# An attention stage whose inverse roots come from one GpSimd power, with the low parts of k made one tile later and in two halves

## The chip, the cores and the metric

The kernel runs on 1 core of one Trainium2 chip. The metric is the device time of one execution in microseconds (us), median of the runs shown; lower is better. The engines are named as the profile names them: PE is TensorE (PEld its weight loads), DVE is VectorE, ACT is ScalarE, POOL is GpSimd, and SP is SyncE, which issues most DMAs.

## The reference, cut to what matters

The whole program is a small network: attention, a mixture of 8 experts, a linear recurrence over the context, and a mixture of 64 experts with two shared ones. The change lies in the first part only:

```python
x = x + jnp.tanh(g_xattn[0]) * _L0_xattn_ref(_layernorm(x, axis=-1), ctx_2048, ctx_2048)
x = x + jnp.tanh(g_ffn[0]) * _L0_ffn_ref(_layernorm(x, axis=-1), L0_ffn_w_gate, ...)

def _layernorm(x, axis=-1, eps=1e-05):
    m = jnp.mean(x, axis=axis, keepdims=True)
    v = jnp.var(x, axis=axis, keepdims=True)
    return (x - m) / jnp.sqrt(v + eps)

def _L0_xattn_ref(q, k, v):            # q, k, v: (4, 512, 512); 8 heads of 64 rows
    attn = jnp.einsum('bct,bcs->bts', qh * scale, kh * scale)
    attn = jax.nn.softmax(attn, axis=-1)
    out = jnp.einsum('bts,bcs->bct', attn, vh)
```

There are 2048 rows of x, 16 tiles of 128 rows. Each tile is normalised, attends, is added back, is normalised again, and its rows are sent to the two experts that a small gate picks.

## The kernel before

The function `attention` holds the stage. It takes the 16 tiles one after another; a tile is 128 rows of x, which are two heads of 64 rows. Every engine runs its own loop over steps i, and in step i the engines work on several tiles at once:

- **PE** computes in step i, in four blocks b of 128 keys, the scores of tile i (L474, L483), the weighted values (L491), and for the next tile i+1 eight "rough" score products m = 0 to 7 (L498), from which only the row maximum is taken. All eight use one PSUM bank, `pM`, so rough m+1 can't start before DVE has read rough m. In between stand the transposes of the normalised tile (L549), those of the values (L554), and the gate's small matmuls (L513, L514, L562). The order of block 0 is: scores, L483, L513 and L514, values of the tile before, rough 0, transposes of `xn`.
- **DVE** takes the negated maximum of each rough product (L661), in the order m = 0 to 7. Between these stand the two halves of a reciprocal (L712), after m = 0 and after m = 1; after m = 3 the statistics of two tiles, of tile i+3 (L719, for the first normalisation) and of tile i-1 (L722, for the second); after m = 5 and 6 the choice of experts (L666 to L681). At the end of the step DVE makes the low parts of q for tile i+2 (L739, two halves, tile `q_parts`), and at the beginning of the next one it computes the slots of a tile's rows (`place`, L687 to L695).
- **ACT** takes the exponentials (L584), copies the softmax sums into `attn` (L590, L591), and at the end of the step rounds q and k to their high parts (L612, L616, tile `k_hi`) and writes the normalised tile `xn` (L622).
- **POOL** goes through an unrolled list: it scatters the rows of tile i-3 by two indirect DMAs (L397), makes q of tile i+2 (L404), finishes the attention of tile i-1 with a product and a sum (L410, L412), turns two variances into inverse roots (L92 to L98), writes the factors of the normalisations (`ln1`, `ln2`: L425, L426), and subtracts the high part of k from k, for tile i+2, in two halves (L437, tile `k_lo`).
- **SP** loads k of tile t (L298, tile `wout`) into one of two slots when the transposes of the values (`vT_full`) and `k_lo` of tile t-2 are done.

The inverse root before: DVE adds the epsilon (L83), shifts the bits right by one (L85) and subtracts them from a constant (L87), which is a first guess. POOL then makes three Newton rounds of four small instructions each (L92, L94, L96, L98), with a drain after each instruction. The two columns of `ve`, `rstd` and `nt` are the two tiles, i-1 and i+3.

A matmul in fp32r takes its operand rounded; `k_hi` and `q_parts` are the rounded parts, `k_lo` and the low parts of q what the rounding left. The scores of tile i need both parts of k; the rough products need `k_hi` and both parts of q.

The order on POOL in step i, as the code has it:

```
scatter(i-3)   q(i+2)   product and sum (i-1)   Newton, ln (i-1, i+3)   k_lo(i+2), both halves
```

The order of the work is written out by hand; the waits are semaphores. PE, ACT and DVE run most steps in a hardware loop of two steps, the first and last ones unrolled.

Of the kernel before, what the change touches and what calls it, by code (L numbers as in the profile page):

```python
# [14 lines left out]
P = 128  # L15
# [21 lines left out]
RSQRT_MAGIC = float(0x5F3759DF)  # L37
# [41 lines left out]


def rsqrt_guess(nc, dve, y, v, half, ve):

    nc.vector.tensor_scalar(ve, v, LN_EPS, None, ALU.add)  # L83
    dve.drain()
    nc.vector.tensor_scalar(half.bitcast(I32), ve.bitcast(I32), 1, None, ALU.logical_shift_right)  # L85
    dve.drain()
    return nc.vector.tensor_scalar(y.bitcast(I32), half.bitcast(I32), -1.0, RSQRT_MAGIC, ALU.mult, ALU.add)  # L87


def newton(ops, eng, y, ve, t):  # L90

    ops.tensor_tensor(t, y, y, ALU.mult)  # L92
    eng.drain()
    ops.tensor_tensor(t, t, ve, ALU.mult)  # L94
    eng.drain()
    ops.tensor_scalar(t, t, -0.5, 1.5, ALU.mult, ALU.add)  # L96
    eng.drain()
    ops.tensor_tensor(y, y, t, ALU.mult)  # L98
    eng.drain()


def rsqrt(nc, dve, y, v, half, scratch):

    ve, t = scratch
    rsqrt_guess(nc, dve, y, v, half, ve)
    dve.drain()
    for _ in range(3):
        nc.vector.tensor_tensor(t, y, y, ALU.mult)
        dve.drain()
        nc.vector.scalar_tensor_tensor(t, t, -0.5, ve, ALU.mult, ALU.mult)  # L110
        dve.drain()
        nc.vector.scalar_tensor_tensor(y, t, 1.5, y, ALU.add, ALU.mult)
        dve.drain()
# [89 lines left out]
def attention(nc, A, T):  # L203
# [6 lines left out]
    with c:  # L210
        def sb(name, shape, dt=F32):
            return c.enter_context(nc.sbuf_tensor(name, shape, dt))

        def sem(name):
            return c.enter_context(nc.semaphore(name))
# [24 lines left out]
        half, ve, nt = sb("half", [P, 2]), sb("ve", [P, 2]), sb("nt", [P, 2])  # L240
# [28 lines left out]
        guess_ready, ln2_ready, xn_ready = sem("guess_ready"), sem("ln2_ready"), sem("xn_ready")  # L269
        ctx_loaded = [sem(f"ctx_loaded_{n}") for n in range(4)]  # L270
        ctx_used, newton_done = sem("ctx_used"), sem("newton_done")
# [91 lines left out]
        def _(pool):  # L363
# [11 lines left out]
            nc.gpsimd.memset(wsel[:], 0.0)  # L375
            nc.gpsimd.iota(iota_e[:], [[1, E1]], base=0, channel_multiplier=0, allow_small_or_imprecise_dtypes=True)
# [14 lines left out]

            for i in range(-3, TILES + 3):
# [7 lines left out]
                if valid(i + 2):  # L400

                    s = i % 2
                    need(pool, q_split, i + 2)
                    nc.gpsimd.tensor_scalar(q[:], x_sb[:, i + 2, :], ln1[:, s, 0:1], ln1[:, s, 1:2],  # L404
                                            ALU.mult, ALU.add).then_inc(q_ready, 1)
                if valid(i - 1):
# [6 lines left out]
                                            ALU.add).then_inc(x1_ready, 1)  # L413
                cols = [n for n, k in enumerate((i - 1, i + 3)) if valid(k)]
                if cols:

                    a, z = cols[0], cols[-1] + 1
                    pool.wait_ge(guess_ready, i + 4)
                    for _ in range(3):
                        newton(nc.gpsimd, pool, rstd[:, a:z], ve[:, a:z], nt[:, a:z])  # L420
# [10 lines left out]
                    nc.gpsimd.engine_nop().then_inc(newton_done, 1)  # L431
# [202 lines left out]
        def _(dve):  # L634
# [62 lines left out]
            def step(i, u, odd):  # L697
# [5 lines left out]
                for m in range(8):  # L703
# [9 lines left out]
                    if m == 3 and cols:  # L713
                        a, z = cols[0], cols[-1] + 1
                        need(dve, newton_done, i + 3)
# [1458 lines left out]
```

## Time and profile before

| | us |
|---|---|
| median of 3 runs | 1229.34 |
| lowest, highest | 1228.84, 1230.68 |
| span of the profiled execution | 1221.8 |
| attention: from the start to the last gate matmul of tile 15 (L514) | 357.7 |
| all that follows | 864 |

The span runs from the first to the last instruction on the core; a run's time holds some 7.5 us more, around it. Over the span PE is busy 88%, DVE 58%, POOL 49%, ACT 40%. A "busy" share of PE is modelled from pipelined matmuls and isn't PE at its peak. In what follows step 5 stands for the steps that repeat; it begins at 120.14 us, with the first L483 of tile 5, and step 6 begins at 140.11. Of an instruction that several engines could release, the trace names the one that came last.

### The profile page before, as it was taken

What the parts mean: (1) busy time and instruction counts of PE and PEld (TensorE: products, weight loads), DVE (VectorE), ACT (ScalarE), POOL (GpSimd) and SP (SyncE); (2) the same over time, 40 slices, a digit from 0 to 9 for tenths busy, and PEclk for the clock granted to TensorE, in tenths of its full rate; (3) what the DMA queues carried; (4) which work ended last, traced back from release to release, by engine and by line L of the source; (5) the groups of instructions that cost most, each with busy time, mean ns of one, the idle gap of its engine ahead of it and who ended that gap; (6) DMA issues with size and microseconds to landing.
All of it is one profiled execution on the core that took longest, in us unless ns stands there. A gap on an engine that the chain in (4) does not pass through costs nothing. (4 is left out here: it accounts for less than half of the span.)

```text
span 1221.8 us, 19314 instructions
## 1 busy us (share of the span) xinstructions
PE 1070.8 (88%) x5503; PEld 752.8 (62%) x5503; DVE 706.4 (58%) x1598; ACT 494.6 (40%) x874; POOL 600.0 (49%) x742
## 2 busy tenths in 40 slices
PE   3999989899856999999788989999997999999930
PEld 2555555555425777777358748677586777788720
DVE  4678888878524888888377616546231333343426
ACT  2565555655404888888433022212211222222200
POOL 5465555656433666666542555647250434343530
PEclk9999999999987999999899989999998999999975
DMA  9854356534165333333440212022025999899739
GB/s 309 298 193 142 135 191 226 183 117 153 63 212 180 100 108 104 103 104 102 168 152 6 78 55 83 26 80 75 5 67 207 365 347 312 279 309 352 199 73 365
DMA packets 115968, 202.39 MB, mean 166 GB/s; under 512 B 19847, under 2 KB 28039, under 8 KB 115898
## 3 DMA queue, kind: packets, MB, share of 16 engines
q1 hardware_dynamic: 95802, 167.47, 40.0%
q0 software_dynamic: 20096, 34.08, 10.0%
q8 instruction: 33, 0.54, 0.2%
q14 instruction: 37, 0.30, 0.1%
HBM read 133.36 MB, written 87.03 MB: 180 GB/s over the span
## 5 line engine op out<-in xcount | busy, mean ns | idle before, releaser
L1959 POOL DMA_INDIRECT sums<-summary,m_token x64 | 99.1, 1549 | 163.2 <-DMA sums<-summary,m_token 81.3
L973 POOL TENSOR_TENSOR m_down_lo<-wo,m_down_hi 128x512 fp32r<-128x512 f32 x80 | 133.3, 1686 | 80.7 <-ACT m_down_hi L1048 80.7
L491 PE MATMUL bank<-win,vT 128*128 128x512 f32 x256 | 124.1, 597 | 0.0
L661 DVE TENSOR_REDUCE negmax<-bank 128x1 bf16<-128x512 f32 x128 | 86.9, 679 | 38.8 <-PE bank L498 38.4
L584 ACT ACTIVATE win<-bank 128x512 f32<-128x512 f32 x128 | 69.4, 594 | 97.3 <-PE bank L483 95.1
L1062 DVE TENSOR_TENSOR m_up_lo<-w,m_up_hi 128x1024 fp32r<-128x1024 f32 x80 | 99.2, 1240 | 10.2 <-ACT m_up_hi L1035 8.4
L1272 POOL DMA_INDIRECT tab<-stage_up,slot x64 | 66.4, 1038 | 50.7 <-DVE slot L1607 32.5
L498 PE MATMUL bank<-k_hi,q_parts 128*128 128x512 f32 x128 | 70.8, 553 | 23.2 <-DVE q_parts L739 14.5
L1982 PE MATMUL bank<-y,m_w 128*128 128x128 f32 x736 | 89.7, 275 | 0.0
L1982 PEld LDWEIGHTS bank<-y,m_w 128*128 128x128 f32 x736 | 86.4, 193 | 0.5 <-issue 0.5
L2137 PE MATMUL bank<-w_sd,stage_gate 128*128 128x512 f32 x192 | 84.9, 598 | 0.3 <-DVE stage_gate L2127 0.3
L2123 ACT ACTIVATE sh_gate_a<-bank 128x512 f32<-128x512 f32 (+1 forms) x40 | 20.5, 512 | 152.4 <-PE bank L2116 112.6
L2033 DVE TENSOR_SCALAR summary<-bank,m_weight 128x512 f32<-128x512 f32 x64 | 48.1, 751 | 54.0 <-DMA sums<-summary,m_token 29.7
L2007 ACT COPY y<-bank 128x512 f32<-128x512 f32 x64 | 37.5, 586 | 101.3 <-PE bank L1974 81.8
L2116 PE MATMUL bank<-flat_hi,w_hi 128*128 128x512 f32 (+1 forms) x320 | 74.6, 356 | 3.9 <-DVE flat_lo L1660 2.2
L2116 PE MATMUL bank<-flat_hi,w_lo 128*128 128x512 f32 (+1 forms) x320 | 72.6, 349 | 1.6 <-issue 1.6
L994 PE MATMUL bank<-m_up_hi,m_xT_hi 128*128 128x512 f32 x160 | 70.1, 438 | 4.2 <-DVE m_up_lo L1062 4.2
L2116 PE MATMUL bank<-flat_lo,w_hi 128*128 128x512 f32 (+1 forms) x320 | 73.0, 351 | 0.0
L498 PEld LDWEIGHTS bank<-k_hi,q_parts 128*128 128x128 f32 x128 | 24.8, 194 | 75.2 <-DVE negmax L661 40.7
L2020 DVE TENSOR_TENSOR m_gh<-m_gh,bank 128x128 f32<-128x128 f32 x64 | 18.3, 286 | 89.3 <-ACT m_gh L2011 65.7
L994 PE MATMUL bank<-m_up_lo,m_xT_hi 128*128 128x512 f32 x160 | 63.7, 398 | 0.0
L994 PE MATMUL bank<-m_up_hi,m_xT_lo 128*128 128x512 f32 x160 | 63.4, 396 | 0.0
(289 smaller groups left out, 2481.6 us busy)
## 6 DMA issues: line engine op xcount, KB each, us to landing
tab<-zeros SPq DMA_DIRECT2D x16, 1056.0 KB
m_w<-in_L_ffn_Wg SPq DMA_DIRECT2D x46, 256.0 KB
m_w<-in_L_ffn_Wu SPq DMA_DIRECT2D x46, 256.0 KB
m_w<-in_L_ffn_Wd SPq DMA_DIRECT2D x46, 256.0 KB
m_x<-tab SPq DMA_DIRECT2D x40, 256.0 KB, 2.6
ytab<-m_y SPq DMA_DIRECT2D x40, 256.0 KB, 2.0
stage_up<-tab SPq DMA_DIRECT2D x32, 264.0 KB
m_x<-tab SPq DMA_DIRECT2D x32, 264.0 KB
```

The costliest lines, as they stand in the source:

```text
L491: nc.tensor.matmul(pO[s * 2 + h][:], vT[:, s, sb_, h:h + 2, :].rearrange("p a c -> p (a c)"), probs[:, sb_ % 2, h, :], start=(sb_ == 0), s ...
L498: nc.tensor.matmul(pM[:], q_parts[:, s, h, t * P:t * P + P], k_hi[:, s, h, :], start=True, stop=True).then_inc(pm_full, 1)
L584: nc.scalar.activation(probs[:, b % 2, h, :], pS[h][:], ACT.Exp, scale=1.0 / HEAD).then_inc(p_ready, 1)
L661: nc.vector.tensor_reduce(negmax[:, s, m:m + 1], pM[:], AX.X, ALU.max, negate=True).then_inc(pm_read, 1)
L973: nc.gpsimd.tensor_tensor(dn_lo[:, m, :], row(wo0, e * MB + m), dn_hi[:, m, :], ALU.subtract).then_inc(dn_lo_ready, 1)
L994: last = nc.tensor.matmul(pH[s][:], x[:, s, d, :], w[:, d, :], start=(d == 0 and part == 0), stop=(d == DB - 1 and part == 2))
L1062: nc.vector.tensor_tensor(up_lo[:, at, :], blocks(w01, e * DB + half * HALF, HALF), up_hi[:, at, :], ALU.subtract).then_inc(up_lo_ready, 1)
L1272: nc.gpsimd.indirect_dma_start(T["tab1"], bass.IndirectOffsetOnAxis(slot1[:, j, k:k + 1], 0), flat[:, j, :], None, bounds_check=E1 * CAP1 ...
L1959: nc.gpsimd.indirect_dma_start(T["sums1"][e % SUMS], bass.IndirectOffsetOnAxis(token[:, e % META:e % META + 1], 0), y[:, e % RING, :], Non ...
L1982: last = nc.tensor.matmul(pH[s][:, k * CAP1:(k + 1) * CAP1], w[:, b, :], xT[:, s, b, :], start=(b == 0), stop=(b == DB - 1))
L2116: last = nc.tensor.matmul(out, w[:, k, s, wc], x[:, d, cols], start=(d == 0 and part == 0), stop=(d == DB - 1 and part == 2))
L2137: last = nc.tensor.matmul(pY[j][:], self.h[:, n, j * P:j * P + P], sd[:, s, b, :], start=(n == 0), stop=(n == self.CHUNKS - 1))
```

## The change

- DVE makes only the sum with epsilon (`ve`); the shift and the subtraction (L85, L87) go. The semaphore is now called `var_ready`.
- POOL raises `ve` to the power -0.5 in one instruction, with a tile `power0` that holds -0.5 (one memset more at the start). The twelve Newton instructions and their drains go. The same instruction on the same engine is already used later in this program, at L1252.
- `k_lo` is made for tile i+1 in step i, where it was made for tile i+2. Its first half stands between q(i+2) and the product of tile i-1, its second half between the sum of tile i-1 and the power.
- A function `rsqrt` that nothing calls goes.

```diff
-                    pool.wait_ge(guess_ready, i + 4)
-                    for _ in range(3):
-                        newton(nc.gpsimd, pool, rstd[:, a:z], ve[:, a:z], nt[:, a:z])
+                    pool.wait_ge(var_ready, i + 4)
+                    nc.gpsimd.tensor_tensor(rstd[:, a:z], ve[:, a:z], power[:, a:z], ALU.pow)
+                    pool.drain()
...
+            def low_half(k, h):
+                s = k % 2
+                pool.wait_ge(k_hi_ready, k + 1)
+                last = nc.gpsimd.tensor_tensor(k_lo[:, s, h, :], kd[:, s, h, :], k_hi[:, s, h, :], ALU.subtract)
+                if h:
+                    last.then_inc(k_lo_ready, 1)
...
+                if valid(i + 1):
+                    low_half(i + 1, 0)
                 if valid(i - 1):
                     ...
+                if valid(i + 1):
+                    low_half(i + 1, 1)
...
-                if valid(i + 2):
-
-                    s = i % 2
-                    pool.wait_ge(k_hi_ready, i + 3)
-                    for h in range(2):
-                        last = nc.gpsimd.tensor_tensor(k_lo[:, s, h, :], kd[:, s, h, :], k_hi[:, s, h, :], ALU.subtract)
-                    last.then_inc(k_lo_ready, 1)
...
-                        rsqrt_guess(nc, dve, rstd[:, a:z], mv[:, a:z, 1], half[:, a:z], ve[:, a:z]).then_inc(guess_ready, 1)
+                        nc.vector.tensor_scalar(ve[:, a:z], mv[:, a:z, 1], LN_EPS, None, ALU.add).then_inc(var_ready, 1)
```

POOL, from the end of one step's list into the next one, before (ahead of the first row stand eleven more Newton instructions):

```order
L98 TENSOR_TENSOR rstd<-rstd,nt 128x2
L425 COPY ln2<-rstd 128x1 [waits xn_ready]
L426 TENSOR_SCALAR ln2<-mv,rstd 128x1
L425 COPY ln1<-rstd 128x1
L426 TENSOR_SCALAR ln1<-mv,rstd 128x1
L431 ISA
L437 TENSOR_TENSOR k_lo<-wout,k_hi 128x512 [waits k_hi_ready]
L437 TENSOR_TENSOR k_lo<-wout,k_hi 128x512
L397 DMA tab0<-xn,slot0 18432x512 [waits slot_ready]
L397 DMA tab0<-xn,slot0 18432x512
L404 TENSOR_SCALAR q<-x_sb,ln1 128x512 [waits q_split]
L410 TENSOR_TENSOR attn<-attn,numer 128x512 [waits recip_ready,po_read]
```

The same engine and place with the change, beginning with the sum of a tile (the lines are those of the changed kernel: L385 is the product, L387 the sum, L361 a half of `k_lo`, L396 the power):

```order
L387 TENSOR_TENSOR x_sb<-x_sb,attn 128x512
L361 TENSOR_TENSOR k_lo<-wout,k_hi 128x512 [waits k_hi_ready]
L396 TENSOR_TENSOR rstd<-ve,power0 128x2 [waits var_ready]
L402 COPY ln2<-rstd 128x1 [waits xn_ready]
L403 TENSOR_SCALAR ln2<-mv,rstd 128x1
L402 COPY ln1<-rstd 128x1
L403 TENSOR_SCALAR ln1<-mv,rstd 128x1
L408 ISA
L370 DMA tab0<-xn,slot0 18432x512 [waits slot_ready]
L370 DMA tab0<-xn,slot0 18432x512
L377 TENSOR_SCALAR q<-x_sb,ln1 128x512 [waits q_split]
L361 TENSOR_TENSOR k_lo<-wout,k_hi 128x512 [waits k_hi_ready]
```

Nothing stands any more between the factors `ln1`, `ln2` and the wait for the next tile's slots; the two halves of `k_lo` stand on either side of the product and the sum.

DVE, the statistics after the maximum m = 3 in the loop's steps, before:

```order
L719 ISA [waits newton_done]
L719 BN_STATS bn<-x_sb 128x6
L722 ISA [waits x1_ready]
L722 BN_STATS bn<-x_sb 128x6
L725 BN_AGGR mv<-bn 128x2 x2
L83 TENSOR_SCALAR ve<-mv 128x2
L85 TENSOR_SCALAR half<-ve 128x2
L87 TENSOR_SCALAR rstd<-half 128x2
L51 REGISTER_ALU
L661 TENSOR_REDUCE negmax<-bank6 128x1 [waits pm_full]
```

and with the change:

```order
L689 ISA [waits ln_done]
L689 BN_STATS bn<-x_sb 128x6
L692 ISA [waits x1_ready]
L692 BN_STATS bn<-x_sb 128x6
L695 BN_AGGR mv<-bn 128x2 x2
L697 TENSOR_SCALAR ve<-mv 128x2
L50 REGISTER_ALU
L631 TENSOR_REDUCE negmax<-bank6 128x1 [waits pm_full]
```

Two small instructions are gone from between the statistics and the maximum m = 4. On PE, ACT and SP the order of the instructions stays as it was.

## Rows read from the trace of the kernel before

**Rows 1.** Windows, steps 3 to 11, then 12 to 14: window, length, busy time by engine.

```profile
81.16:257.66 176.50, 161.77 (x846) 95.12 (x847) 143.89 (x316) 99.22 (x181) 103.28 (x207) 1.00 0.52 180
257.66:314.37 56.71, 54.17 (x282) 31.81 (x282) 45.70 (x101) 30.81 (x57) 33.65 (x64) 1.00 0.40 141
```

**Rows 2.** Waits in the first 400 us: who waited for whom, us, times, longest.

```profile
PE bank L498 <- DVE q_parts L739: 14.5, 11, 4.6
```

**Rows 3.** Durations in ns (min/median/max) of L739 on DVE and L437 on POOL.

```profile
L739 DVE TENSOR_TENSOR q_parts<-q,q_parts x32: 684/1656/1778, 14.9 to 297.0; 64x512 fp32r<-64x512 f32 x32
ACT q_parts L612: 0.5, 1
...
L437 POOL TENSOR_TENSOR k_lo<-wout,k_hi x32: 1260/1634/1779, 20.2 to 296.4; 128x512 fp32r<-128x512 f32 x32
```

**Rows 4.** Timeline of step 5: start, duration in us, engine, line, [idle before <- releaser].

```profile
120.06 2.94 POOL L437 TENSOR_TENSOR k_lo<-wout,k_hi 128x512 fp32r<-128x512 f32 x2 [0.18 <-issue]
120.12 3.43 DVE L739 TENSOR_TENSOR q_parts<-q,q_parts 64x512 fp32r<-64x512 f32 x2
120.14 0.62 PE L483 MATMUL bank<-identb,negmax 128*128 128x128 bf16 x8 [0.44 <-DVE negmax L661]
...
120.66 1.96 PE L491 MATMUL bank<-win,vT 128*128 128x512 f32 x4
...
123.31 0.58 ACT L591 COPY attn<-bank 64x512 f32<-64x512 f32 x1
...
123.69 0.50 PE L498 MATMUL bank<-k_hi,q_parts 128*128 128x512 f32 x1 [1.07 <-DVE q_parts L739]
...
125.37 1.75 DVE L712 RECIPROCAL attn<-attn 128x256 f32<-128x256 f32 x1
```

**Rows 5.** The same timeline further on, from q to the statistics of tile 4.

```profile
127.20 0.76 POOL L404 TENSOR_SCALAR q<-x_sb,ln 128x512 f32<-128x512 f32 x1
...
127.76 1.75 DVE L712 RECIPROCAL attn<-attn 128x256 f32<-128x256 f32 x1
...
129.66 1.28 POOL L410 TENSOR_TENSOR attn<-attn,numer 128x512 f32<-128x512 f32 x1 [1.70 <-DVE attn L712]
...
131.25 1.27 POOL L412 TENSOR_TENSOR x_sb<-x_sb,attn 128x512 f32<-128x512 f32 x1 [0.32 <-issue]
...
131.40 0.68 DVE L719 BATCH_NORM_STATS2 bn<-x_sb 128x6 f32 x1
...
132.74 0.69 DVE L722 BATCH_NORM_STATS2 bn<-x_sb 128x6 f32 x1 [0.65 <-POOL x_sb L412]
```

**Rows 6.** The same timeline, from the sum with epsilon to the factors.

```profile
133.83 0.17 DVE L83 TENSOR_SCALAR ve<-mv 128x2 f32<-128x2 f32 x1
...
134.35 0.62 PE L483 MATMUL bank<-identb,negmax 128*128 128x128 bf16 x8
134.44 0.69 DVE L661 TENSOR_REDUCE negmax<-bank 128x1 bf16<-128x512 f32 x1
134.57 0.20 POOL L92 TENSOR_TENSOR nt<-rstd 128x2 f32<-128x2 f32 x1 [2.04 <-DVE rstd L87]
...
135.19 0.50 PE L498 MATMUL bank<-k_hi,q_parts 128*128 128x512 f32 x1 [0.21 <-DVE negmax L661]
...
138.89 0.19 POOL L425 COPY ln<-rstd 128x1 f32<-128x1 f32 x1
```

**Rows 7.** Groups by shape on POOL, 600 to 870 us: the power; busy us, mean ns.

```profile
L1252 POOL TENSOR_TENSOR rstd<-ve,power 128x2 f32<-128x2 f32 x6 | 4.3, 714 | 21.1 <-DVE ve L1624 21.1
```

**Rows 8.** Timeline of PE: rough 0 of tile 0 and of tile 1.

```profile
16.43 0.77 PE L498 MATMUL bank<-k_hi,q_parts 128*128 128x512 f32 x1 [4.61 <-DVE q_parts L739]
...
32.85 0.50 PE L498 MATMUL bank<-k_hi,q_parts 128*128 128x512 f32 x1 [1.31 <-DVE q_parts L739]
```

**Rows 9.** Timeline of PE behind the last values: transposes of the normalised tile 14.

```profile
332.31 0.63 PE L549 MATMUL bank<-ident,xn 128*128 128x128 f32 x4 [2.11 <-ACT xn L622]
```

**Rows 10.** Loads of k (L298) by SP: from issue to landing.

```profile
DMA to landing us min/median/max: 2.4/2.7/9.0
```

More of the change, by code:

```diff
@@ L78, in steps @@
         step(i, i // ring, i % ring)
[L81 to L106, printed above, removed]
-    for _ in range(3):
[L108 to L113, printed above, removed]
 def build(nc, A, out):
@@ L239, in attention @@
         rstd = sb("rstd", [P, 2])
-        half, ve, nt = sb("half", [P, 2]), sb("ve", [P, 2]), sb("nt", [P, 2])
+        ve, power = sb("ve", [P, 2]), sb("power0", [P, 2])
         ln1 = sb("ln1", [P, 2, 2])
@@ L268, in attention @@
         q_hi_ready, q_split, recip_ready = sem("q_hi_ready"), sem("q_split"), sem("recip_ready")
-        guess_ready, ln2_ready, xn_ready = sem("guess_ready"), sem("ln2_ready"), sem("xn_ready")
+        var_ready, ln2_ready, xn_ready = sem("var_ready"), sem("ln2_ready"), sem("xn_ready")
         ctx_loaded = [sem(f"ctx_loaded_{n}") for n in range(4)]
-        ctx_used, newton_done = sem("ctx_used"), sem("newton_done")
+        ctx_used, ln_done = sem("ctx_used"), sem("ln_done")
         vT_full, vT_ready = sem("vT_full"), sem("vT_ready")
@@ L375, in _ @@
             nc.gpsimd.memset(wsel[:], 0.0)
+            nc.gpsimd.memset(power[:], -0.5)
             nc.gpsimd.iota(iota_e[:], [[1, E1]], base=0, channel_multiplier=0, allow_small_or_imprecise_dtypes=True)
@@ L417, in _ @@
                     a, z = cols[0], cols[-1] + 1
-                    pool.wait_ge(guess_ready, i + 4)
-                    for _ in range(3):
-                        newton(nc.gpsimd, pool, rstd[:, a:z], ve[:, a:z], nt[:, a:z])
+                    pool.wait_ge(var_ready, i + 4)
+                    nc.gpsimd.tensor_tensor(rstd[:, a:z], ve[:, a:z], power[:, a:z], ALU.pow)
+                    pool.drain()
                     for n, ln in ((0, ln2[:, (i - 1) % 2]), (1, ln1[:, (i + 3) % 2])):
@@ L430, in _ @@
                     pool.drain()
-                    nc.gpsimd.engine_nop().then_inc(newton_done, 1)
-                if valid(i + 2):
-                    s = i % 2
-                    pool.wait_ge(k_hi_ready, i + 3)
-                    for h in range(2):
-                        last = nc.gpsimd.tensor_tensor(k_lo[:, s, h, :], kd[:, s, h, :], k_hi[:, s, h, :], ALU.subtract)
-                    last.then_inc(k_lo_ready, 1)
+                    nc.gpsimd.engine_nop().then_inc(ln_done, 1)
             for s in range(2):
@@ L714, in step @@
                         a, z = cols[0], cols[-1] + 1
-                        need(dve, newton_done, i + 3)
+                        need(dve, ln_done, i + 3)
                         if valid(i + 3):
```

1 line of the change is left out of this document (removed).

## Prediction

> **What bounds the kernel now.** The change touches the attention stage, the first 358 of 1221.8 us, so only this stage is read; what follows it starts when it ends and keeps its length. I read first the windows over the repeating steps [rows 1]. Steps 3 to 11 take 176.5 us, 19.6 us each, steps 12 to 14 take 56.7 us, 18.9 each. PE is modelled as busy 92% there, and its clock is the full one (1.00). So PE is near its limit but isn't all of it: about 1.6 us of a step are waits.
>
> The waits say for whom: PE's first rough product of a step waits for the low parts of q, which DVE makes (14.5 us, 11 times) [rows 2]. Why are these late? One half of L739 takes 684 ns at best and 1656 ns in the median; a half of `k_lo` on POOL takes 1260 at best and 1634 in the median [rows 3]. The timeline of step 5 shows both at the same time: `k_lo` begins at 120.06 and `q_parts` at 120.12, and the pair on DVE takes 3.43 us where two halves alone take 1.37 [rows 4]. The two engines hold each other up. DVE loses 2.06 us there, POOL 0.42. PE ends its values at 122.62 (120.66 + 1.96) and idles 1.07 us for rough 0.
>
> From there I follow the step, in us from its start at 120.14. Rough 0 is issued at 3.55; DVE first has to place a tile, then takes maximum 0, and starts the first reciprocal at 5.23, though ACT had delivered its input at 3.75 (123.31 + 0.58) [rows 4]. The second reciprocal starts at 7.62; POOL's product follows it at 9.52, its sum at 11.11, DVE's statistics of that sum at 12.60 after a wait of 0.65 [rows 5]. Then come `ve` at 13.69, maximum 4 at 14.30, and PE's rough 5 at 15.05, after a wait of 0.21 for it [rows 6]. So this is one chain from `q_parts` to rough 5: DVE, POOL, DVE, PE. Behind rough 5 the order is rigid (three rough products, each waiting for the maximum before, and the choice of experts): the remaining 4.6 us stay.
>
> **The change, part by part.**
>
> *`k_lo` leaves q_parts.* In the new order POOL has nothing to read between the factors and the next slots, so `q_parts` takes 1.37 to 1.40 us. DVE places its tile 2 us earlier, but the first reciprocal can't start before its input at 3.75; with rough 0 issued at 2.5, right behind the values, maximum 0 is read by about 3.75 too. I take 3.85, which is 1.4 us earlier than 5.23.
>
> *First half, in front of the product.* Between q (ends 127.96) and the product (129.66) POOL waits 1.70 us for the second reciprocal [rows 5]. Half a `k_lo` takes 1.26 alone [rows 3]: it fits, with 0.4 to spare, and more since the slots come 2 us earlier and the reciprocal only 1.4. If the cover were gone it would cost up to 1.26 in each step, on the chain.
>
> *Second half, behind the sum.* It runs 1.26 us, from the sum's end at 132.52 to 133.78 on the old clock, where DVE's `ve` starts at 133.83 [rows 5, 6]; POOL has to wait for `ve` anyway. It costs nothing, at most 0.1. It runs beside the statistics of the same tile. Whether those are held up is bounded by a neighbour: at 131.40 the other statistics (L719) ran inside POOL's sum, 0.68 us against 0.69 for the ones that ran alone, and the sum kept its 1.27 [rows 5]. So between 0 and, by the hold of `q_parts`, 1.0; I take 0.
>
> *Two DVE instructions go.* `ve` at 13.69, maximum 4 at 14.30: 0.61 us with three instructions, 0.15 with one. That is 0.45 earlier for maximum 4.
>
> *Twelve Newton instructions become one power.* Newton runs from 134.57 to 138.89, 4.3 us [rows 6]; the power on two columns takes 0.71 [rows 7], 0.9 with its drain. In a repeating step the 3.4 us are worth nothing, since the factors feed ACT's `xn` and the q of two steps on, both off the chain. They count where the stage is short of work: at its start and end.
>
> **What is late next.** By DVE's chain rough 5 could be issued 1.4 + 0.45 earlier, at 13.2. But PE itself needs from rough 0 to the L483 of block 3 134.35 - 123.69 = 10.66 us, with hardly a wait inside, and 0.45 more for these matmuls [rows 4, 6]: 2.5 + 10.66 + 0.45 = 13.6. The later one decides, PE. So the step gains 15.05 - 13.6, rounded down to 1.4 us, and about 0.4 us of slack is left on DVE's chain. Steps 12 to 14 are already 0.7 us shorter [rows 1] and meet the same limit, so they gain 0.7.
>
> **The sum.**
> - Steps 3 to 11: 9 x 1.4 = 12.6.
> - Steps 12 to 14: 3 x 0.7 = 2.1.
> - Step 0: PE waits 1.31 for the overlapped `q_parts` [rows 8], and no values stand in front of it: 1.3.
> - Start: rough 0 of tile 0 waits until 16.43 for `q_parts` [rows 8], which came behind two guess instructions (0.45) and a wait of 0.5 for ACT [rows 3], whose q hangs on Newton, now 3.9 us earlier: 0.9.
> - In steps -1 and 1, without the slot work, the 0.45 us at maximum 4 reach PE: 1.0 together, an estimate.
> - End: the transposes of tile 14 wait 2.11 us for `xn`, behind Newton [rows 9]; with 3.4 + 0.45 us less there the wait goes whole, and the expert choice ahead comes 0.45 sooner: 2.5.
>
> Together 20.4 us. The profiled span becomes 1201.4, and the time 1229.3 - 20.4 = 1208.9, taken against the median with the same 7.5 us around the span.
>
> The trace shows no first use of the power in this stage. The Trainium skill (GPSIMD Engine Reference, section 2.1, Instruction dispatch) says that the first call to a freshly loaded GpSimd kernel pays about 6 us more. It would fall on the power near 7 us; `q_parts` of tile 0 would come some 2 us later than I have it, and the sum would be 18.5. The row of the power's later uses, 714 ns in the mean, shows no such load.
>
> **Rivals.**
> - *PE isn't the limit* (13%). If the 10.66 us contain hidden waits for DVE, rough 5 comes at 13.2, and 12 steps gain 0.4 to 0.45 more: 1204. For it: pM serialises rough 1 and 2 with DVE. Against it: in step 5 no wait above 0.2 us stands between them.
> - *The second half holds the statistics* (12%). With 1.0 us on the chain rough 5 comes at 14.2, and 12 steps lose 0.6 to 0.65: 1216. Against it stands L719 inside the sum.
> - *Slower: the hold moves with `k_lo`* (5%). Today the overlap costs DVE 2.06 and POOL 0.42 us, of which 1.4 reach the chain. If the reciprocals and the statistics are held up as `q_parts` is, all 2.5 fall on it, on both sides of the product: rough 5 at 13.2 + 2.5 = 15.7, 0.65 later than now. Nine steps lose 5.9, three lose 4.1 (1.35 each), start and end gain 5.7: 1233.6. It decides against the change from a hold of about 1.9 us in each step. For it: the same two engines and memory. The Trainium skill (SBUF — State Buffer, Who interferes with whom) says that a DVE instruction with two SBUF inputs contends with GpSimd's reads and one with a single input doesn't, outside the two-port modes; by that rule `q_parts` is held, the statistics are not, and the time is my forecast. Against it without the rule: L719 again, and 1.75 us for both reciprocals, one of which overlaps q.
> - *The change doesn't do what it says* (5%): `q_parts` meets other work. The second half now ends near 12.3 us of the step and `q_parts` begins at 18, so POOL would have to slip by 6 us. Or the loads of k, issued 3.5 us later in a step since they wait for `k_lo`, come late: they land in 2.7 us, 9.0 at most [rows 10], against some 20 us until they are read. About 1229.
>
> **How the numbers follow.** Forecast 65%, 1205 to 1213; the rivals as above. Eight in ten are held from 1203 to 1217. Faster by over 0.2%, which is about what a measurement of this kernel can tell from no change, has 90%: forecast and the first two rivals. Within 0.2%: 4%. Slower: 6%.
>
> **What would show it.** L739 near 0.69 us and L437 near 1.27 throughout; the wait of L498 for L739 down to the one at the start; steps of 18.2 us; rough 5 of a step at 13.6 with no wait for maximum 4; the power at 0.71; no wait of L549 at the end; the later stages shifted but not shortened. It is wrong if L712, L722 or L410 grow, if POOL's product starts behind `k_lo` and not behind the reciprocal, or if ACT waits for loads of k.

## The result and the profile after

| | before | after |
|---|---|---|
| time, median (runs) | 1230.01 us (1228.84 to 1232.51) | 1205.83 us (1205.41 to 1205.94) |
| span of the profiled execution | 1221.8 us | 1203.8 us |
| ratio | | 0.983 (95%: 0.981 to 0.985) |

The changed kernel is 24 us faster by the medians of the first comparison, and by 21.9 and 19.8 us in two later ones on other occasions. Between the two profiled executions lie 18.0 us. The last matmul that counts experts for tile 15 is the end of the stage. It is at 357.72 us before and at 340.13 after, 17.6 us earlier, so all but 0.4 us of the 18.0 arose in the attention stage. The start of that matmul, in PE's timeline of the changed kernel, is the ruler for most of what follows:

```profile
340.13 0.17 PE L484 MATMUL bank<-chosen,onesb 128*128 128x8 bf16 x1
```

What comes behind it took 860 to 867 us in the profiled executions of this study, though nothing was edited there.

The windows of the changed kernel over the same steps as [rows 1], and over the end (window, length, busy us by engine, PE clock, DMA share, GB/s):

```profile
78.85:244.31 165.46, 158.04 (x846) 95.59 (x846) 123.19 (x298) 98.65 (x180) 84.29 (x108) 1.00 0.59 200
244.31:298.26 53.95, 52.20 (x283) 31.81 (x283) 39.53 (x95) 30.60 (x56) 26.30 (x31) 1.00 0.43 148
298.26:340.13 41.87, 34.61 (x143) 14.95 (x144) 15.10 (x58) 13.10 (x23) 13.18 (x16) 0.95 0.50 164
```

Steps 3 to 11 take 165.5 us in place of 176.5, 18.4 us each. The durations that answer to [rows 3] (ns, min/median/max), and who still waited for the low parts of q, as in [rows 2]:

```profile
L709 DVE TENSOR_TENSOR q_parts<-q,q_parts x32: 684/686/689, 14.0 to 281.1; 64x512 fp32r<-64x512 f32 x32
PE bank L468: 3.4, 1
...
L361 POOL TENSOR_TENSOR k_lo<-wout,k_hi x32: 1255/1276/1295, 16.6 to 291.3; 128x512 fp32r<-128x512 f32 x32
```

The longest `q_parts` is now within 5 ns of the shortest before, and `k_lo` has a spread of 40 ns where it had 519. Of 14.5 us that PE waited for `q_parts`, only the wait in front of tile 0 is left.

The mean step hides that there are two kinds. First the timeline of step 6, an even one, which starts at 134.62:

```profile
134.59 1.39 DVE L709 TENSOR_TENSOR q_parts<-q,q_parts 64x512 fp32r<-64x512 f32 x2
...
135.13 1.96 PE L461 MATMUL bank<-win,vT 128*128 128x512 f32 x4
...
136.53 0.79 PE L468 MATMUL bank<-k_hi,q_parts 128*128 128x512 f32 x1
...
142.81 1.28 POOL L385 TENSOR_TENSOR attn<-attn,numer 128x512 f32<-128x512 f32 x1 [1.10 <-DVE attn L682]
144.40 1.27 POOL L387 TENSOR_TENSOR x_sb<-x_sb,attn 128x512 f32<-128x512 f32 x1 [0.32 <-issue]
145.62 1.28 POOL L361 TENSOR_TENSOR k_lo<-wout,k_hi 128x512 fp32r<-128x512 f32 x1
145.90 0.69 DVE L692 BATCH_NORM_STATS2 bn<-x_sb 128x6 f32 x1 [0.68 <-POOL x_sb L387]
147.11 0.69 DVE L631 TENSOR_REDUCE negmax<-bank 128x1 bf16<-128x512 f32 x1
147.51 0.62 PE L453 MATMUL bank<-identb,negmax 128*128 128x128 bf16 x8
147.94 0.48 PE L468 MATMUL bank<-k_hi,q_parts 128*128 128x512 f32 x1
```

Rough 5 (147.94) stands 13.3 us into the step without a wait. Then the same stretch of step 5, an odd one, which starts at 115.73:

```profile
123.80 1.28 POOL L385 TENSOR_TENSOR attn<-attn,numer 128x512 f32<-128x512 f32 x1 [1.02 <-DVE attn L682]
126.64 1.27 POOL L387 TENSOR_TENSOR x_sb<-x_sb,attn 128x512 f32<-128x512 f32 x1 [1.56 <-issue]
...
128.12 0.69 DVE L692 BATCH_NORM_STATS2 bn<-x_sb 128x6 f32 x1 [1.78 <-POOL x_sb L387]
...
130.08 0.50 PE L468 MATMUL bank<-k_hi,q_parts 128*128 128x512 f32 x1 [0.84 <-DVE negmax L631]
```

The product is as early as in step 6 (8.1 us in), but the sum starts 1.56 us after it instead of 0.32. The statistics come 1.1 us later in the step, rough 5 waits 0.84 us and stands at 14.35. The profile gives that gap to "issue", which names no one. Between the two instructions stands only GpSimd's drain. No step of the kernel before has such a gap ([rows 5]: 0.32). Where does it come from?

### The profile page after: what moved, and what is told of

Read it like the earlier page. It is cut to its first block and busy times, and to the rows that moved or that the text cites. A ratio compares the mean times of both kernels' runs of the same rounds, so it can differ in the third digit from the quotient of the medians.

```text
span 1203.8 us, 18795 instructions
## 1 busy us (share of the span) xinstructions
PE 1067.6 (89%) x5503; PEld 756.9 (63%) x5503; DVE 673.7 (56%) x1558; ACT 493.5 (41%) x874; POOL 555.4 (46%) x523
## 3 DMA queue, kind: packets, MB, share of 16 engines
q0 software_dynamic: 20096, 34.08, 10.2%
## 5 line engine op out<-in xcount | busy, mean ns | idle before, releaser
L461 PE MATMUL bank<-win,vT 128*128 128x512 f32 x256 | 124.1, 597 | 0.0
L1032 DVE TENSOR_TENSOR m_up_lo<-w,m_up_hi 128x1024 fp32r<-128x1024 f32 x80 | 98.9, 1238 | 10.2 <-ACT m_up_hi L1005 8.4
L468 PE MATMUL bank<-k_hi,q_parts 128*128 128x512 f32 x128 | 76.2, 595 | 12.7 <-DVE negmax L631 9.2
L2093 ACT ACTIVATE sh_gate_a<-bank 128x512 f32<-128x512 f32 (+1 forms) x40 | 20.4, 512 | 153.7 <-PE bank L2086 139.9
L370 POOL DMA_INDIRECT tab<-xn,slot x32 | 32.8, 1024 | 103.1 <-DVE slot L665 98.2
L2107 PEld LDWEIGHTS bank<-w_sd,stage_gate 128*128 128x128 f32 x192 | 36.7, 194 | 43.3 <-issue 43.2
## 6 DMA issues: line engine op xcount, KB each, us to landing
tab<-zeros SPq DMA_DIRECT2D x16, 1056.0 KB, 11.8
```

Of the source, the lines that this page charges most:

```text
L461: nc.tensor.matmul(pO[s * 2 + h][:], vT[:, s, sb_, h:h + 2, :].rearrange("p a c -> p (a c)"), probs[:, sb_ % 2, h, :], start=(sb_ == 0), s ...
L468: nc.tensor.matmul(pM[:], q_parts[:, s, h, t * P:t * P + P], k_hi[:, s, h, :], start=True, stop=True).then_inc(pm_full, 1)
L1032: nc.vector.tensor_tensor(up_lo[:, at, :], blocks(w01, e * DB + half * HALF, HALF), up_hi[:, at, :], ALU.subtract).then_inc(up_lo_ready, 1)
L2107: last = nc.tensor.matmul(pY[j][:], self.h[:, n, j * P:j * P + P], sd[:, s, b, :], start=(n == 0), stop=(n == self.CHUNKS - 1))
```

## The experiments

All are edits of the changed kernel. The lengths of steps, taken from one first matmul of L453 (it turns maximum 0) to the next in each trace, and the end of the stage (all in us; "even" and "odd" are the medians of steps 4 to 12 and 3 to 11):

| kernel | time, median | even | odd | tile 15's step starts | end of stage |
|---|---|---|---|---|---|
| before | 1225.1 / 1226.5 / 1227.4 | 19.5 | 19.7 | 314.37 | 357.72 |
| changed | 1204.6 / 1207.6 | 17.84 | 18.9 | 298.26 | 340.13 |
| pow_only | 1211.3 | 18.9 | 18.9 | 306.75 | 347.79 |
| klo_only | 1213.3 | 18.15 | 19.5 | 305.42 | 349.87 |
| bulk_even | 1204.0 | 18.8 | 17.84 | 297.54 | 339.46 |
| sum_wait | 1198.6 / 1201.3 | 17.84 | 17.84 | 292.61 | 334.80 |
| guess_back | 1209.3 | 18.15 | 19.7 | 305.89 | 347.53 |
| both_front | 1203.9 | 17.88 | 18.8 | 298.07 | 340.12 |
| scatter_late | 1201.3 | 18.2 | 18.1 | 296.95 | 340.51 |
| klo_wait | 1210.3 | 17.9 | 18.0 | 296.42 | 345.35 |

Three medians of before belong to three comparisons: the first to `pow_only`, `klo_only`, `bulk_even` and the first `sum_wait`; the second to `guess_back`, `both_front`, `scatter_late` and the first time of changed; the third to the rest. The steps and ends of changed are those of the first profile. Each end of the stage is that of one profiled execution: the three profiles of the changed kernel have it at 340.13, 339.81 (`after_again`) and 338.67 (`after5`), and the profiled execution of `guess_back` (1213.3) and that of `scatter_late` (1203.8) were the slowest of their four. So 1 to 1.5 us in this column can be chance.

**Each half of the change alone.** `pow_only` takes both halves of `k_lo` back to the end of the step:

```diff
-                if valid(i + 1):
-                    low_half(i + 1, 0)
...
-                if valid(i + 1):
-                    low_half(i + 1, 1)
...
                     nc.gpsimd.engine_nop().then_inc(ln_done, 1)
+                if valid(i + 2):
+                    low_half(i + 2, 0)
+                    low_half(i + 2, 1)
```

> The power stays, both halves of k_lo go back to the end of GpSimd's step for tile i + 2. By the theory of the prediction the start (the rounds' 2.2 us that stood in front of tile 0) is won as in the changed kernel, and k_lo, which now starts when k_hi is there rather than behind twelve small instructions, meets VectorE's q_parts with about half of its length: q_parts in mid-run at 1.0 to 1.4 us in place of 1.66 to 1.78 before and 0.69 in the changed kernel, time 1210 to 1213 us. If the whole collision stays (q_parts 1.6 and over), only start, end and the last steps are won: 1219 to 1225 us. A further point: the scatter is again queued behind k_lo and so issued as late as before. If what makes GpSimd stand 1.2 to 1.8 us between product and sum in the odd steps of the changed kernel is its own early scatter, there is no such gap here (0.3 us in all steps); if it is the code's place or the bulk loads by themselves, it is there.

It took 1211.3 us, ratio 0.990 (0.987 to 0.993): within the first theory's range, though from a before of 1225.1 that is a gain of 13.7, less than the range meant (16 to 19 from the 1229.3 that it was taken against). `q_parts` has a median of 1.08 us, as the first theory had it. In the timeline of its step 6 the collision is a partial one, and it costs in proportion:

```profile
135.89 2.50 POOL L361 TENSOR_TENSOR k_lo<-wout,k_hi 128x512 fp32r<-128x512 f32 x2 [2.79 <-ACT k_hi L585]
137.83 1.81 DVE L708 TENSOR_TENSOR q_parts<-q,q_parts 64x512 fp32r<-64x512 f32 x2
```

They overlap for 0.56 us and `q_parts` is 0.43 longer than its 1.38. In [rows 4] they overlapped for 2.88 us and it was 2.06 longer. The gap between product and sum is 0.32 to 0.38 us in all its steps with a scatter.

`klo_only` puts the Newton rounds and VectorE's guess back and leaves `k_lo` in its new places:

```diff
-                    nc.gpsimd.tensor_tensor(rstd[:, a:z], ve[:, a:z], power[:, a:z], ALU.pow)
-                    pool.drain()
+                    for _ in range(3):
+                        newton(nc.gpsimd, pool, rstd[:, a:z], ve[:, a:z], nt[:, a:z])
...
-                        nc.vector.tensor_scalar(ve[:, a:z], mv[:, a:z, 1], LN_EPS, None, ALU.add).then_inc(var_ready, 1)
+                        rsqrt_guess(nc, dve, rstd[:, a:z], mv[:, a:z, 1], half[:, a:z], ve[:, a:z]).then_inc(var_ready, 1)
```

> Newton rounds and guess are as before the change, k_lo stands in its two new places. By the theory of the prediction the collision of k_lo with q_parts is gone (q_parts 0.69 us throughout), start and end are those of before: gain 10 to 16 us, 1214 to 1220 us. If the power's shorter chain carried the gain in the steps, q_parts is short here and the time still stays above 1222 us. The scatter is issued as early as in the changed kernel; if that is what makes the gap between product and sum, odd steps show 1.2 to 1.8 us here too.

1213.3 us, ratio 0.991 (0.989 to 0.994): a gain of 11.8, within the 10 to 16 of the first theory; as a time it lies 0.7 us below the range of 1214 to 1220. `q_parts` is short (684/687/689 ns), and the gaps of the odd steps are there (1.27 to 1.75 us in steps 3 to 13). By the ends of the stage `k_lo` alone brings 7.9 us, the power alone 9.9, and together they bring 17.6: nearly a plain sum. By the medians it is 11.8 and 13.7, against 19.8 to 24.2 for both in three comparisons. So each alone is worth roughly half; how much of it they share isn't settled.

**Whose gap is it.** `bulk_even` changes only when SyncE issues the block of weight loads and zeroing:

```diff
                     load_k(sp, t, n)
-                behind(u)
+                    if n == 0:
+                        behind(u)
```

> The changed kernel with one edit: SyncE's block of weight loads and zeroing (some 4.8 MB, once in two tiles) is issued after the even tile's k instead of the odd tile's. Theory: the drain between GpSimd's product and sum lasts until the scatter issued at the head of the step has gone through, and the block holds the scatter up. Then the gaps of 1.2 to 1.8 us move from the odd steps (3, 5, 7 ...) to the even ones, with VectorE's wait at the roughs' end (0.4 to 0.9 us), and the time stays within 3 us of the changed kernel's (1203 to 1209 us). Rival, the instructions' place in GpSimd's code: the gaps stay in the odd steps.

The gaps moved. The sum of steps 4, 5 and 6 of `bulk_even` on GpSimd's timeline:

```profile
106.78 1.27 POOL L388 TENSOR_TENSOR x_sb<-x_sb,attn 128x512 f32<-128x512 f32 x1 [1.10 <-issue]
124.43 1.27 POOL L388 TENSOR_TENSOR x_sb<-x_sb,attn 128x512 f32<-128x512 f32 x1 [0.32 <-issue]
143.57 1.27 POOL L388 TENSOR_TENSOR x_sb<-x_sb,attn 128x512 f32<-128x512 f32 x1 [1.47 <-issue]
```

So it isn't the place in the code. Having the block in the step isn't enough either: `pow_only` has it, issued earlier, and has no gap. Whether the scatter comes into it is the next question. `scatter_late` moves the scatter behind the sum and leaves block and drain where they are:

```diff
-                if valid(i - 3):
-                    pool.wait_ge(slot_ready, i - 2)
-                    for k in range(2):
-                        nc.gpsimd.indirect_dma_start(
...
                                             ALU.add).then_inc(x1_ready, 1)
+                if valid(i - 3):
+                    pool.wait_ge(slot_ready, i - 2)
+                    for k in range(2):
+                        nc.gpsimd.indirect_dma_start(
...
                 if valid(i + 1):
                     low_half(i + 1, 1)
```

> The changed kernel with the scatter of tile i - 3 issued behind the sum instead of at the head of GpSimd's step; the drain between product and sum stays, and so do the bulk loads. If that drain waits for the scatter, the gap between product and sum is 0.3 us in all steps, odd ones too, and what stands still in the odd steps is now the next drain behind the scatter, the one between the power and the copies of its result (over 1 us against 0.3 in the even steps). If a drain is slow under the bulk loads whatever was issued, the gap between product and sum stays at 1.2 to 1.8 us in the odd steps. The time is no test here: the two issues (2 x 1.0 us) now stand in front of the power, and tile i - 1's xn waits for them; 1200 to 1225 us.

GpSimd's timeline of step 5 of `scatter_late` (odd) and, behind the dots, the power of step 6:

```profile
124.00 1.27 POOL L378 TENSOR_TENSOR attn<-attn,numer 128x512 f32<-128x512 f32 x1 [5.00 <-DVE attn L682]
125.42 1.27 POOL L380 TENSOR_TENSOR x_sb<-x_sb,attn 128x512 f32<-128x512 f32 x1
126.86 1.07 POOL L386 DMA_INDIRECT tab<-xn,slot  x1 [0.17 <-issue]
128.24 0.97 POOL L386 DMA_INDIRECT tab<-xn,slot  x1 [0.30 <-issue]
129.23 1.29 POOL L361 TENSOR_TENSOR k_lo<-wout,k_hi 128x512 fp32r<-128x512 f32 x1
130.47 0.73 POOL L396 TENSOR_TENSOR rstd<-ve,power 128x2 f32<-128x2 f32 x1
133.36 0.18 POOL L402 COPY ln<-rstd 128x1 f32<-128x1 f32 x1 [2.17 <-issue]
...
148.92 0.74 POOL L396 TENSOR_TENSOR rstd<-ve,power 128x2 f32<-128x2 f32 x1
149.97 0.18 POOL L402 COPY ln<-rstd 128x1 f32<-128x1 f32 x1 [0.31 <-issue]
```

The sum follows its product after 0.15 us (124.00 + 1.27 to 125.42), and what stands still now is the next drain behind the scatter, for 2.17 us. That is what the first theory said. It was not quite the pattern: step 4, an even one, has 2.04 us there too, and step 3 only 0.32. In step 3 the scatter was issued 14.3 us behind the block and had landed when the power ended. In step 4 the block was issued only at 115.20, after the scatter had landed (114.83), so what held that scatter was not the block, and no run shows what it was. In both steps 4 and 5 the copy starts 0.20 us after the landing. The time, 1201.3 us, is 3.2 under the changed kernel beside it, though the stage of the profiled execution ends no earlier (340.51).

The list of DMA issues closes the loop. From issue to landing (median us, the last number), the scatter of steps 5 and 6 of `after_again`, an unedited run of the changed kernel:

```profile
tab<-xn,slot POOLq DMA_INDIRECT x2, 6.2
...
tab<-xn,slot POOLq DMA_INDIRECT x2, 2.8
```

In that step 5 the second scatter was issued at 118.83. With 6.2 us it landed at 125.06, and the sum began at 125.27, 1.1 us behind its product. In step 7 it was issued at 155.12, landed at 161.73, and the sum began at 161.94. The trace has a row of the drain itself too, from 122.85 in step 5:

```profile
L386 POOLq DRAIN  x1: 2329/2329/2329, 122.9 to 122.9; - x1
```

It ends at 125.18, 0.12 us after the landing and 1.0 us after the product. In all six odd steps of `after_again`, of `klo_only`, `guess_back` and `both_front`, and in the five even ones of `bulk_even` with a gap, the sum begins 0.21 to 0.22 us after the second scatter has landed, whatever the gap is. With 2.8 us the scatter has long landed when the product ends. In step 5 of `pow_only` the block was issued 12 us ahead of the scatter rather than 5.3, the second scatter took 4.6 us from 123.42, and it landed 0.3 us before the product ended at 128.32: no gap.

**Take the wait away.** `sum_wait` gives the sum a semaphore that only the product raises:

```diff
-                    nc.gpsimd.tensor_tensor(attn[:], attn[:], numer[:], ALU.mult)
-                    pool.drain()
+                    nc.gpsimd.tensor_tensor(attn[:], attn[:], numer[:], ALU.mult).then_inc(x1_ready, 1)
+                    pool.wait_ge(x1_ready, 2 * i - 1)
...
-                        need(act, x1_ready, i - 1)
+                        need(act, x1_ready, 2 * (i - 1))
...
-                            need(dve, x1_ready, i, alone=1)
+                            need(dve, x1_ready, 2 * i, alone=2)
```

> The changed kernel, with the drain between GpSimd's product and sum replaced by a semaphore that the product itself raises and that GpSimd waits for (x1_ready, which now counts two per tile). Theory: the drain waits for the scatter too, a semaphore of the product alone does not; the gaps of 1.2 to 1.8 us in the odd steps fall to that of the even ones (0.3 us), the odd steps get shorter by 0.4 to 0.9 us, six of them, and the time falls to 1199 to 1203 us. Rival, the sum itself or its code is late (the bulk transfers in the way of its operands or of its instructions): the gap stays and the time with it, 1205 to 1207 us.

> The changed kernel again, unedited, as the measure for the two beside it: 1203 to 1206 us, even steps of 17.84 us, odd ones near 18.8.

> The version with the semaphore in place of the drain again, beside the changed kernel on one chip. The six odd steps from 3 to 13 lose 0.6 to 1.1 us each, all steps are 17.8 to 17.96 us: 5.0 to 6.5 us under the changed kernel, 1197 to 1200 us. If the earlier lead came from the chip or the day, the two are within 2 us.

1198.6 us against 1225.1 for before (0.980, 0.977 to 0.983), 0.4 below the range of the theory. In the comparison side by side it took 1201.3 (1199.7 to 1205.6) and the changed kernel 1207.6 (1206.7 to 1208.5), 6.3 us apart, within the 5.0 to 6.5 expected. Both times lie 1.3 to 1.6 us above the ranges given for them, and one run of five of the first lies near the second. Product and sum of step 5 of `sum_wait`, and the window over steps 3 to 11 of `sum_wait5`:

```profile
122.43 1.28 POOL L385 TENSOR_TENSOR attn<-attn,numer 128x512 f32<-128x512 f32 x1 [1.03 <-DVE attn L682]
...
123.79 1.27 POOL L387 TENSOR_TENSOR x_sb<-x_sb,attn 128x512 f32<-128x512 f32 x1
```

```profile
78.69:239.27 160.58, 156.99 (x847) 95.35 (x847) 123.14 (x298) 98.66 (x180) 84.18 (x108) 1.00 0.60 205
```

0.08 us between them, and the steps from 3 on are 17.8 to 18.0 us, most of them 17.84, 98% of it PE. The stage ends at 334.80 and 334.33. This version beats both kernels.

**How much slack VectorE has.** `guess_back` adds only VectorE's two small instructions, on a spare tile:

```diff
-                        nc.vector.tensor_scalar(ve[:, a:z], mv[:, a:z, 1], LN_EPS, None, ALU.add).then_inc(var_ready, 1)
+                        nc.vector.tensor_scalar(ve[:, a:z], mv[:, a:z, 1], LN_EPS, None, ALU.add)
+                        dve.drain()
+                        nc.vector.tensor_scalar(half[:, a:z].bitcast(I32), ve[:, a:z].bitcast(I32), 1, None,
+                                                ALU.logical_shift_right)
+                        dve.drain()
+                        nc.vector.tensor_scalar(half[:, a:z].bitcast(I32), half[:, a:z].bitcast(I32), -1.0, 1.0,
+                                                ALU.mult, ALU.add).then_inc(var_ready, 1)
```

> The changed kernel itself, unedited, as the measure for the three beside it on this chip. Expected 1204 to 1206 us, with the gaps between product and sum in the odd steps again.

> The changed kernel with the guess's two small VectorE instructions put back behind the sum of the variance (they now work on a spare tile), 0.45 us more on VectorE in each step before the negmax of rough 5. By the theory that PE limits the even steps with some 0.4 us to spare while VectorE limits the six odd ones with a gap, this costs 6 x 0.45 = 2.7 us in the odd steps and almost nothing in the others: 2 to 4 us over the changed kernel run beside it. If PE limits everywhere it costs nothing (within 1 us); if VectorE is the limit in every step, 11 x 0.45 = 5 us and more.

`after_again` took 1204.6 us, `guess_back` 1209.3. It cost 4.8 us in time and 7.7 in the stage (347.53 against 339.81), more than was expected. Even steps are 0.31 us longer: 0.45 were added and 0.14 were slack. Odd steps grew by 0.9: 0.45 were added without any slack, the gap itself was 0.2 longer (medians of 1.69 and 1.50), and the rest isn't explained. In step 5 rough 5 waited 1.40 us:

```profile
132.76 0.50 PE L468 MATMUL bank<-k_hi,q_parts 128*128 128x512 f32 x1 [1.40 <-DVE negmax L631]
```

1.9 us more had piled up by the start of step 2, in steps that the expectation had left out. From `klo_only` (349.87) to `guess_back` (347.53) lies what replacing the Newton rounds themselves brings, about 2.3 us, and from there to the changed kernel what the two VectorE instructions bring, 7.7. By the medians, each against its own kernel before, the same two are 5.3 (gains of 11.8 and 17.1) and 4.8, so this split is uncertain by some 3 us. By time alone the third theory of the expectation, 5 us and more, fits as well as the first; the even steps, which grew by less than 0.45, speak for the first.

`klo_wait` prices the same without the gaps (`klo_only` with the edit of `sum_wait`):

> k_lo in its new places with Newton rounds and guess as before the change, and the semaphore in place of the drain. It prices the power without the gaps. Theory: the 0.45 us of the guess lie on VectorE's chain, which is 0.14 us shorter than PE's without them, so each step is 17.84 + 0.31 = 18.15 us, odd and even alike, ten such steps give 181.5 us, and the start is 1.0 us later (rough 0 of tile 0 at 16.4): 5 to 7 us over the kernel with semaphore and power beside it, 1203 to 1206 us. Rival: Newton's 3.4 us lie on a chain in the steps too, then a step is 18.5 us and over, and the time 1208 us or more.

The steps are 17.9 (even) and 18.0 (odd), not 18.15. The sum semaphore saves 0.2 us in every step, as it also removes the 0.32 us of the short drain, so VectorE's slack is nearly the guess's 0.45. The time, 1210.3, missed the range, and the steps were shorter than either theory had them. The stage's end, 345.35, shows where: 3.8 us against `sum_wait5` until tile 15's step, and 7.2 behind it, where ACT's `xn` of tile 14 waits for Newton and PE then waits up to 2.2 us at a time for the context loads. Why the loads come late there wasn't tried. Waits are 4.6 of the 7.2 us. The rest is PE's own busy time, at a lower granted clock. The stretch from tile 15's step to the end of the stage, of `klo_wait` and of `sum_wait5`:

```profile
296.42:345.35 48.93, 38.17 (x144) 16.54 (x144) 15.70 (x62) 13.36 (x24) 16.52 (x38) 0.86 0.43 140
...
292.64:334.33 41.69, 35.57 (x143) 15.05 (x144) 15.13 (x58) 13.12 (x23) 13.16 (x16) 0.94 0.50 164
```

In `klo_wait` the clock falls to its lower level (0.5 of full, 1.2 GHz) at 314.49 for 3.4 us, behind PE's wait of 2.34 us for `xn`, and again at 334.96, behind the wait of 2.20 us; in `sum_wait5` only at 328.97. So 1210.3 prices the power together with this, and not the power alone.

**The cover of the first half.** `both_front` puts both halves of `k_lo` ahead of the product:

> The changed kernel with both halves of k_lo in front of the product. GpSimd waits 1.10 us there for the reciprocals in a step of mid-run, so the second half (1.28 us) pushes product and sum 0.2 us back and leaves room behind the sum. Theory that the hole in front of the product is nearly long enough: even steps keep their length (the 0.4 us of slack takes it), odd ones, limited by the sum, get 0.2 longer, 0 to 2 us over the changed kernel run beside it. Rival: the first half had hidden nothing in that hole and the second costs its whole 1.3 us in every step, 10 us and more over it.

1203.9 us against 1204.6 for the changed kernel beside it, stage end 340.12 against 339.81: no difference. The product starts 8.31 us into step 6 (141.82 - 133.51) rather than 8.19. GpSimd's wait ahead of the product covers nearly both halves; the second half's place behind the sum brought next to nothing. The odd steps did not get the expected 0.2 us longer (18.8). With both halves done early, SyncE issued its block 9.3 to 10.2 us ahead of the scatter, and the gaps stayed (1.17 to 1.45 us).

## Why the prediction was right, point by point

The time, 1205.8, lies inside the forecast's own range, and the mechanism named was the one at work. That the time came so close is in part luck: an overlooked loss, a gain per step that was too small and a wrong account of the span offset each other, as the points below show. Of its steps:

| | predicted | measured, profile against profile |
|---|---|---|
| start, to the start of step 3 | 0.9 + 1.0 + 1.3 = 3.2 | 2.3 (81.16 to 78.85) |
| steps 3 to 11 | 12.6 | 11.0 (176.50 - 165.46) |
| steps 12 to 14 | 2.1 | 2.8 (56.71 - 53.95) |
| end | 2.5 | 1.5 (43.35 - 41.87) |
| sum | 20.4 | 17.6 |

- *The collision.* Right, with its price: `q_parts` at 0.69 throughout, and the even steps of `klo_only`, where `k_lo` alone moved, are 1.4 us shorter than before (18.15 against 19.5). The half overlap of `pow_only` confirms the cause. The rival in which the hold moves fell on the rows of step 6: L692, with one input, ran beside `k_lo` and took 0.69 us. The rule of the Trainium skill (SBUF — State Buffer, Who interferes with whom) names two inputs as what makes the difference, and both traces agree with it. One sum of that rival is off: with its own terms the whole change would lose from a hold of 2.15 us in each step; 1.9 is where a repeating step begins to.
- *PE is the next limit.* Right for the even steps, too late by 0.3 us. The prediction had rough 0 at 2.5 us, the end of the record of the values. In step 6 it starts at 1.91, 0.56 us before the record of L461 ends; from there to L453 it is 10.98 instead of 10.66, and rough 5 comes at 13.3 instead of 13.6. An even step is 17.84 us where 18.2 were expected, 1.7 less than before. The Trainium skill (Perfetto Trace Analysis, Tensor Engine Instruction) says that the end of a TensorE record is computed and not observed; the row of L461 agrees.
- *Slack of 0.4 us on VectorE's chain.* With PE's limit earlier it was 0.14 (`guess_back`), and it was negative in the odd steps. VectorE's chain itself was foreseen well: product at 9.52 - 1.4 = 8.12, measured 8.19. The rival "PE isn't the limit" expected this chain at 13.2; it was the level of PE that was lower, not a hidden wait in it.
- *"Where the cover is gone".* The cover held. The step that failed is that of what else moves with `k_lo`; the prediction put it at nothing. The scatter, no longer queued behind `k_lo`, is issued 1.9 to 2.0 us earlier in a step (4.7 before, 2.7 after). The prediction used this as room for the first half. And SyncE's block stands behind the loads of k, which wait for `k_lo`. The prediction had these loads 3.5 us later in a step, and asked only whether they would be late for their readers. The block ahead of step 5, before and changed:

```profile
112.06 1.00 SPq L328 DMA_DIRECT2D w<-in_L_ffn_wi  x2
...
113.08 1.00 SPq L292 DMA_DIRECT2D w<-in_L_ffn_wi  x2
```

  It came 8.1 us ahead of the step and now comes 2.7 ahead, so the scatter of an odd step follows it after 5.3 us instead of 12.8. Of these 7.5 us the block's delay is 5.4, the earlier scatter 2.0. The earlier scatter by itself isn't enough: in `pow_only` it is issued 1.6 us earlier than before, 11.5 to 12.0 us behind the block, and there is no gap; `both_front`, at 9.3 to 10.2 us, has it. What the scatter then meets is the block's traffic, and behind it stands a drain that waits for its landing. That makes odd steps 0.5 to 1.1 us longer than even ones, 5.3 us over six of them. It used up the 0.3 per step that PE gave more, and so the mean step, 18.4, still came out near the 18.2 foreseen.
- *The start.* Rough 0 of tile 0 came 0.91 us earlier, as predicted (0.9). Step -1 and step 1 gave 0.47 and 0.54, as predicted together. Step 0 gave 0.4 and not 1.3 in this profile, but 1.1 in `after_again` and 1.0 in `after5` (14.75 and 14.79 us, 15.82 before). There the whole start, to step 3, gives 3.1 and 3.3 (78.04 and 77.91), which is the 3.2 predicted. In the first profile the wait for `q_parts` is gone too, but the products behind it run slowly:

```profile
30.10 0.78 PE L468 MATMUL bank<-k_hi,q_parts 128*128 128x512 f32 x1
30.68 0.72 PE L444 MATMUL bank<-q_parts,k_hi 128*128 128x512 f32 x1
31.20 0.63 PE L444 MATMUL bank<-q_parts,k_lo 128*128 128x512 f32 x1
31.62 0.63 PE L444 MATMUL bank<-q_parts,k_hi 128*128 128x512 f32 x1
32.05 0.46 PE L444 MATMUL bank<-q_parts,k_lo 128*128 128x512 f32 x1
```

  Against 0.40 in mid-run. The trace's record of the granted clock, at 1.00, begins only at 32.18 us; ahead of it there is no record, and the 1.00 that a window prints there is no reading. In `after_again` the record begins at 30.18, and the matmuls of L444 behind it take 0.40. In all 13 traces the record begins between 30.2 and 34.6 us and the long rows end there, so the granted clock is the cause as far as the rows tell; that it stood at its lower level ahead of the record is argued. In the kernel before, the record begins at 31.22, inside the wait, and so the first matmul behind the wait was a short one ([rows 8], 0.50 at 32.85). In the first profile and in `after_again` PE had waits of 0.8 to 1.0 us between roughs until 27 us and none from there on. Why the rise comes 2 us earlier in some executions isn't shown.
- *The end.* Tile 14's transposes have no wait (L519 at 313.80, 15.5 us behind the step's start where it was 17.9): 2.4, as predicted. Behind them 0.9 us went back. From there to the end of the stage, before and changed:

```profile
332.31:357.72 25.41, 18.93 (x64) 5.43 (x64) 8.22 (x32) 4.93 (x9) 9.13 (x20) 0.96 0.79 247
...
313.80:340.13 26.33, 19.48 (x64) 6.10 (x63) 7.92 (x30) 5.05 (x9) 7.16 (x9) 0.92 0.74 239
```

  PE's waits, mostly for the context loads, grew by 0.4 us and its busy time by 0.55, with a mean clock of 0.92 instead of 0.96. The clock fell to its lower level 4.2 us ahead of the stage's end (at 335.97, behind a wait of 1.81 us) and before the change 2.2 us ahead (at 355.49, behind one of 1.80).
- *The power.* 0.72 us in the mean on two columns, 0.63 on one. The first one, at 6.96 us, took 0.58, behind a wait of 2.21 us for `ve`, and the copy of its result followed at 7.69. The Trainium skill (GPSIMD Engine Reference, Instruction dispatch) gives a first call to a freshly loaded kernel about 6 us more; this trace shows no such cost at the power, and no run shows whether the power counts as freshly loaded there.
- *The account around the span.* The prediction added 7.5 us to the span of before. Each run lists time and span, and they are 1.8 to 2.0 us apart; the rest was the profiled execution being shorter than the median. With 17.6 and 2.0 in the place of 20.4 and 7.5 the result would have been 1206.2. The two errors partly offset each other, which is luck. The gain itself was 24.2 us by the medians of the first comparison and 21.9 and 19.8 in the later ones, so 20.4 lies within what was measured, and 17.6 is what one pair of profiles gives.

## What to carry to other kernels

When an instruction moves, ask of every instruction that was queued behind it, and of every one that waits for its result on another engine, what it meets at its new time; here a block of transfers came 5.4 us later and a scatter 2.0 us earlier, and the scatter landed 0.9 to 1.5 us behind the product that it used to precede. Between two dependent operations on an engine that also issues indirect DMAs, wait for a semaphore of the first operation rather than drain the engine: here that was worth 6 us. And read an engine's slack from the starts of its neighbours' instructions, since 0.3 us in the level of the limit decided whether two 0.17 us instructions cost nothing or, as here, about 5 us (4.8 in the medians, 7.7 in one pair of profiles).

## What the runs showed of the hardware

- A drain on GpSimd waits until the scatters that GpSimd issued have landed, not only for its arithmetic: in all six odd steps of `after_again` the sum began 0.21 to 0.22 us after the landing, 1.1 to 1.7 us behind its product. With a scatter already landed the gap between two dependent operations is 0.32 us. With none in front it is 0.15 (`scatter_late`, 125.42 against 124.00 + 1.27), with a semaphore 0.08.
- A scatter of 2 x 128 rows (0.52 MB by the software queue, two issues of 1.07 and 0.97 us) lands 2.7 to 2.8 us after issue in the steps of `after_again` without the block and 6.0 to 6.7 us in those with it, where the queues move about 400 GB/s. Issued 11.5 to 12.0 us behind the block (`pow_only`) it takes 4.3 to 5.1 us. The Trainium skill (Perfetto Trace Analysis, DMA Instruction — SWDGE (GPSIMD)) says that the row's end is the end of the making of descriptors and not of the transfer; this trace agrees, the rows being 1 us long.
- Two instructions that read two tiles of SBUF each, one on VectorE and one on GpSimd, lengthen each other where they overlap: VectorE's pair by 2.06 us over an overlap of 2.88 and by 0.43 over one of 0.56.
